# One neighbour product for group 1, chosen by a predicated copy, and a new order of TensorE's turns

## The chip, the cores and the metric

The kernel runs on one core of one Trainium2 chip. The metric is the device time of one execution in microseconds; the figure quoted is the median over the runs. Times inside the kernel are read from one profiled execution and counted in microseconds from the start of its span.

## The reference

The kernel computes one layer of deformable attention over 8 images of 32 channels and 16 x 16 pixels, then a self-attention, then a mixture of 16 small networks. The change touches only the bias of the first attention. Per image and group (G = 2) a convolution predicts an offset for each of 16 sample points; the bias of a query pixel for a point is a bilinear lookup in a table `rpe` at the distance between the two:

```
pos  = offset + ref_points(Hk, Wk)
disp = (qg - pos) * 0.5
bias = grid_sample(rpe_b, disp[..., ::-1])
attn = softmax(einsum('bcm,bcn->bmn', qf, k) * scale + bias)
```

Along x the query grid advances by a little less than one table column per pixel (fifteen sixteenths). So for query column x the lookup is a sum over three neighbouring columns of the shifted table: `here` with weight 1 - |dist|, the next column with weight max(dist, 0), the previous column with weight max(-dist, 0), where dist = frac - x/16. At least one of the last two weights is always zero.

## The kernel before, in words

All 128 partitions hold (image, point) pairs in an order by x position. For each group g, TensorE (the matmuls of L733) writes the table blended along y into PSUM, `row_ps[g]`: 32 rows (16 query rows by 2 heads) at a pitch of 32 columns, 21 columns of which are written. VectorE moves each partition's rows left by a whole number of columns with three predicated copies (`shifted`, L1101), whose mask is one number per partition. GpSimd computes the masks and the weights `tap_next`, `tap_prev`, `tap_both` (their sum) and `tap_here` (L471 to L488).

Then come the products, each of 128 partitions by 512 elements, built by the helper `tap` (its record is L390):

- Group 0: ScalarE copies the shifted rows to SBUF (`win`, L566), and GpSimd forms `left[0]`, `right[0]`, `here[0]` from the copy. Each raises `part_ready[0]`.
- Group 1: VectorE forms `left[1]`, `right[1]`, `here[1]` straight from PSUM, with no wait between them. Each raises `part_ready[1]`.

TensorE turns every product with transposing matmuls (`turn_on`, L761) and accumulates it into `lg_ps`, the logits. `lg_ps` has one bank for each half h of the query pixels. One `turn_on` is two matmuls (one a head) for one product, one group and one half; so the six products make 24 matmuls. Into the same banks go the products of queries and keys (L783), four matmuls of 256 columns a half. Those wait for `k_ready`: the keys are projected by TensorE (`project(0)`, L754), then ScalarE copies them twice, once a head (L571).

The order is the order in which the code is written; each engine takes its instructions strictly in that order, and a wait holds all that stand behind it. On TensorE it is: keys projected; left and right of group 0 for both halves; left of group 1 for both halves; then for each half the four query-key matmuls, right of group 1, here of group 0, here of group 1, and `logits_done`. After that come the projection of the values (`project(1)`, L754) and eight matmuls on x (L797), and then those on the values (L805), which wait for ScalarE's copies of them.

Behind `logits_done` of a half VectorE takes the maximum over a row (L1130) and subtracts it (L1131), ScalarE takes the exponent, VectorE sums and inverts, and the probabilities of half 0 are formed by GpSimd, those of half 1 by VectorE (L398). TensorE's matmuls on `zeros` (L680) fill waits of known length; they keep the engine busy and compute nothing.

Of the kernel before, what the change touches and what calls it, by code (L numbers as in the profile page):

```python
# [9 lines left out]
U32 = mybir.dt.uint32  # L10
ALU = mybir.AluOpType
ACT = mybir.ActivationFunctionType
AX = mybir.AxisListType

P = 128
B, C = 8, 32
IMG = 16
M = IMG * IMG
NHALF = M // P
G = 2  # L20
GC = C // G
HG = 2
# [8 lines left out]
WIN = IMG + 1 + MAXSHIFT  # L31
# [99 lines left out]
def build(nc, x_in, consts_in, weights_in, w1_in, w2_in, out):  # L131
    with ExitStack() as ctx:
# [9 lines left out]
        def bank(n, cols=512):  # L142
            return ps[:, 512 * n:512 * n + cols]
# [67 lines left out]
        tap_next = sb("tap_next", [P, G, IMG])  # L211
        tap_prev = sb("tap_prev", [P, G, IMG])
        tap_both = sb("tap_both", [P, G, IMG])
        tap_here = sb("tap_here", [P, G, IMG])
        win = sb("win", [P, IMG * HG, IMG + 1])

        here = sb("here", [P, G, HG, IMG, IMG])
        left = sb("left", [P, G, HG, IMG, IMG])
        right = sb("right", [P, G, HG, IMG, IMG])
# [56 lines left out]
        row_ps = [ps[:, 1024 * g:1024 * g + 1024].rearrange("p (r c) -> p r c", c=RPAD) for g in range(G)]  # L276
# [8 lines left out]
        sq_ps = [bank(n, M) for n in (4, 2)]  # L285
        y_ps = [bank(n, M) for n in (1, 5)]

        qpad_ps = [bank(2 + g, PADIMG * PADIMG).rearrange("p (y x) -> p y x", y=PADIMG) for g in range(G)]
        q_ps = [qpad_ps[g][:, PAD:PAD + IMG, PAD:PAD + IMG] for g in range(G)]
        att_ps = [bank(2 + h, B * C) for h in range(NHALF)]  # L290
# [51 lines left out]
        k_done, v_done, k_ready, v_ready = sem("k_done"), sem("v_done"), sem("k_ready"), sem("v_ready")  # L342
        vo_done, vo_copied = sem("vo_done"), sem("vo_copied")
        rows_done, win_copied = sem("rows_done"), sem("win_copied")
        shifts_done, left_edge_zeroed = sem("shifts_done"), sem("left_edge_zeroed")
        hat_smp_ready = sem("hat_smp_ready")
        part_ready = [sem(f"part_ready{g}") for g in range(G)]
        logits_done, d_sub_ready = sem("logits_done"), sem("d_sub_ready")
# [39 lines left out]
        def tap(engine, product, g, window, shift, weights, x0=0):  # L388

            return engine.tensor_tensor(  # L390
                product[:, g, :, :, x0:], window[:, :, x0 + shift:IMG + shift].rearrange("p (y h) x -> p h y x", h=HG),
                weights[:, g, x0:].unsqueeze(1).unsqueeze(1).to_broadcast([P, HG, IMG, IMG - x0]), ALU.mult)
# [112 lines left out]
        def _(act):  # L505
# [57 lines left out]
            load_table(LN_EXP_SET)  # L563

            act.wait_ge(shifts_done, 1)
            nc.scalar.activation(win[:, :, :], row_ps[0][:, :, 0:IMG + 1], ACT.Copy).then_inc(win_copied, 1)  # L566

            def copy_heads(w, ready):

# [100 lines left out]
        def _(pe):  # L670
            mm = nc.tensor.matmul

            def nx_rows(nx):

                return slice(nx * P // NK, (nx + 1) * P // NK)
# [11 lines left out]
            for g in range(G):  # L687
                for gi in range(G):
                    pe.wait_ge(xn_ready, gi + 1)
                    last = mm(q_ps[g], wblk[:, 0, gi, g].rearrange("p b o -> p (b o)"),  # L690
                              xn[:, gi].rearrange("p (y x) -> p y x", y=IMG), start=(gi == 0), stop=(gi == G - 1))
# [3 lines left out]
            for h in range(NHALF):  # L695
                for g in range(G):
                    last = nc.tensor.transpose(xnt_ps[:, h, g], xn[:, g, h * P:(h + 1) * P], ident)  # L697
# [22 lines left out]
            for g in range(G):  # L720
                for nx in range(NK):
                    last = mm(tx_ps[nx_rows(nx), g:g + 1], off_blk[:, g].rearrange("p b n -> p (b n)")[:, nx::NK],
                              weight("w_off")[:, 1:2], start=True, stop=True)
# [5 lines left out]
            for g in range(G):  # L729
                for yq in range(4):  # L730
                    pe.wait_ge(hat_rel_ready, yq + 1)
                    for nx, least in enumerate(table_columns()[0]):
                        last = mm(row_ps[g][nx_rows(nx), 8 * yq:8 * yq + 8, 0:WIN],  # L733
                                  minus_hat_rel[:, yq, g * P + nx:(g + 1) * P:NK],
                                  rpe_blk[:, g].rearrange("p k (h c) -> p (k h) c", h=HG)[:, :, least:least + WIN],
                                  start=True, stop=True)
                last.then_inc(rows_done, 1)
# [4 lines left out]
            for g in range(G):  # L742
                for h in range(NHALF):
                    last = mm(xs_ps[:, g], xn_tok[:, h, g], w_smp[:, h, g * P:(g + 1) * P],
                              start=(h == 0), stop=(h == NHALF - 1))
# [12 lines left out]
            def turn_on(part, g, h, start=False):  # L758

                for hh in range(HG):  # L760
                    last = mm(lg_ps[:, h, g, :, hh], part[:, g, hh, 8 * h:8 * h + 8].rearrange("p y x -> p (y x)"),  # L761
                              back_to_n[:, :].rearrange("p (t j) -> p t j", t=NT), start=(start and hh == 0),
                              stop=True, is_transpose=True, skip_group_check=True)
                return last
# [2 lines left out]

            pe.wait_ge(back_to_n_ready, 1)
            pe.wait_ge(txh_ready, 1)
            pe.wait_ge(part_ready[0], 1)  # L770
            for h in range(NHALF):
                turn_on(left, 0, h, start=True)
# [1 line left out]
            for h in range(NHALF):  # L774
                turn_on(right, 0, h)

            pe.wait_ge(part_ready[1], 1)
            for h in range(NHALF):
                turn_on(left, 1, h)
            pe.wait_ge(k_ready, HG)  # L780
            for h in range(NHALF):
                for g in range(G):
                    mm(lg_ps[:, h, g].rearrange("p t k j -> p (t k j)"), q_sb[:, g, h * P:(h + 1) * P],  # L783
                       kv[:, 0, g].rearrange("p t k j -> p (t k j)"), start=False, stop=False, skip_group_check=True)
                pe.wait_ge(part_ready[1], 2)
                turn_on(right, 1, h)
                pe.wait_ge(part_ready[0], 3)
                turn_on(here, 0, h)
                pe.wait_ge(part_ready[1], 3)
                turn_on(here, 1, h).then_inc(logits_done, 1)  # L790

            project(1).then_inc(v_done, 1)
            pe.wait_ge(x_nat_loaded, 16 * B)
# [8 lines left out]
            for outputs, blk in ((voc_ps, woblk_c), (vo_ps, woblk)):  # L802
                for g in range(G):
                    for t in range(NT):
                        last = mm(outputs[:, g, t], kv[:, 1, g, t].rearrange("p k j -> p (k j)"),  # L805
                                  blk[:, g, B4 * t:B4 * t + B4].rearrange("p b o -> p (b o)"),
                                  start=True, stop=True)
# [3 lines left out]
            for h in range(NHALF):  # L811
                pe.wait_ge(d_prob_ready[h], 1)
                for g in range(G):
                    for t in range(NT):
                        first = 2 * B * g + B * t
                        last = nc.tensor.transpose(
                            pt_ps[:, h, g, t], d_prob[:, h, first:first + B].rearrange("p b n -> p (b n)"), ident)
# [4 lines left out]
            for h in range(NHALF):  # L822
                pe.wait_ge(prob_copied, h + 1)
                for t in range(NT):
                    for g in range(G):
                        last = mm(att_ps[h][:, P * t:P * t + P], prob_t[:, h, g, t], vo_c[:, g, t],  # L826
                                  start=False, stop=(g == G - 1), skip_group_check=True)
# [93 lines left out]
            for h in range(NHALF):  # L921
                for b in range(B4, B):
                    last = score(late_ps[:, b - B4, h], b, h, start=(h == 0))
# [3 lines left out]
            for h in range(NHALF):  # L927
                for b in range(B4):
                    last = attend(early_ot_ps, b, h, slice(0, M), start=(h == 0), stop=(h == 1))
            last.then_inc(ot_done, 1)  # L930
            pe.wait_ge(folded_ready, 2)
            for b in range(B4):
                last = add_up(early_sum_ps, b, e_fold[:, b], start=False, stop=True)
# [9 lines left out]
            for q in range(NHALF):  # L943
                queries = slice(P * q, P * q + P)
                pe.wait_ge(exp_ready, NHALF + 2 + q + 1)
                for b in range(B4, B):
                    last = add_up(late_sums_ps[:, q], b, e_tok[:, b, 1, queries], start=False, stop=True)
                last.then_inc(sums_done, 1)
                for b in range(B4, B):
                    last = attend(late_ot_ps[q], b, 1, queries, start=False, stop=True)  # L950
# [47 lines left out]
            for h in range(NHALF):  # L998
                pe.wait_ge(u_copied, 1)
                pe.wait_ge(picked_copied, h + 1)  # L1000
                for b in range(B):
                    last = mm(pool_ps[:, NE * b:NE * b + NE], u[:, h, b, :], picked_t[:, h, b::B],
                              start=(h == 0 and b == 0), stop=(h == NHALF - 1), skip_group_check=True)
# [5 lines left out]
            for q in range(EQ):  # L1009
                last = mm(hid_ps[:, q].rearrange("p e b -> p (e b)"), w1_sb[:, q, :],  # L1010
                          pooled[:, q].rearrange("p e b -> p (e b)"), start=False, stop=True,
                          skip_group_check=True)
# [7 lines left out]
            for e in range(E4):  # L1020
                for q in range(EQ):
                    last = mm(out2_ps[E4 * B * q:E4 * B * q + E4 * B],
                              hidden_blk[:, q, e].rearrange("p f b -> p (f b)"), w2_sb[:, E4 * q + e],
                              start=False, stop=(e == E4 - 1), skip_group_check=True)
# [9 lines left out]
        def _(dve):  # L1034
            steps = [0]

            def link(ins):
                steps[0] += 1
                ins.then_inc(dve_step, 1)
                dve.wait_ge(dve_step, steps[0])  # L1040
# [58 lines left out]
            def shifted(g, width, mask, by):  # L1099

                return nc.vector.copy_predicated(  # L1101
                    row_ps[g][:, :, 0:width], mask.bitcast(U32).unsqueeze(2).to_broadcast([P, IMG * HG, width]),
                    row_ps[g][:, :, by:by + width])

            dve.wait_ge(masks_ready, 1)
            dve.wait_ge(rows_done, 1)
# [12 lines left out]

            dve.wait_ge(shifts_done, 2)  # L1120
            dve.wait_ge(taps_ready, 1)
            dve.wait_ge(left_edge_zeroed, 1)
            tap(nc.vector, left, 1, row_ps[1], -1, tap_prev, 1).then_inc(part_ready[1], 1)
            tap(nc.vector, right, 1, row_ps[1], 1, tap_next).then_inc(part_ready[1], 1)
            tap(nc.vector, here, 1, row_ps[1], 0, tap_here).then_inc(part_ready[1], 1)

            lg_rows = [lg_ps[:, h].rearrange("p g t k (b n) -> p (g t k b) n", n=N) for h in range(NHALF)]
            for h in range(NHALF):
# [162 lines left out]
```

## Time and profile before

| | |
|---|---|
| median of 3 runs | 60.37 us (60.14, 60.37, 61.9) |
| the profiled execution's own time | 59.97 us |
| its span (first to last instruction) | 58.0 us |
| TensorE matmul busy | 50.6 us (87%), 603 matmuls |
| VectorE busy | 36.9 us (64%) |
| ScalarE busy | 29.9 us (52%) |
| GpSimd busy | 18.4 us (32%) |
| transfers | 2.02 MB, 35 GB/s mean |

The profiled execution took 59.97 us, of which 58.0 are the span; 1.97 us lie around it. Busy time counts matmuls as they are modelled: they are pipelined, so the records overlap, and the filling matmuls on `zeros` count too. What a matmul costs in a stream is therefore read from the distance between the starts of two groups, not from its own duration. TensorE's granted clock is at its full level in all 40 slices of the page.

### The profile page before, as it was taken

What the parts mean: (1) busy time and instruction counts of PE and PEld (TensorE: products, weight loads), DVE (VectorE), ACT (ScalarE), POOL (GpSimd) and SP (SyncE); (2) the same over time, 40 slices, a digit from 0 to 9 for tenths busy, and PEclk for the clock granted to TensorE, in tenths of its full rate; (3) what the DMA queues carried; (4) which work ended last, traced back from release to release, by engine and by line L of the source; (5) the groups of instructions that cost most, each with busy time, mean ns of one, the idle gap of its engine ahead of it and who ended that gap; (6) DMA issues with size and microseconds to landing.
All of it is one profiled execution on the core that took longest, in us unless ns stands there. A gap on an engine that the chain in (4) does not pass through costs nothing.

```text
span 58.0 us, 1496 instructions
## 1 busy us (share of the span) xinstructions
PE 50.6 (87%) x603; PEld 41.8 (72%) x603; DVE 36.9 (64%) x95; ACT 29.9 (52%) x66; POOL 18.4 (32%) x41
## 2 busy tenths in 40 slices
PE   3996996999699699999999999979999998979720
PEld 3995894985388579899898986726688675867500
DVE  3478399775659989449994046739267866785320
ACT  0802052787999903104744785197984639801020
POOL 6130089995878899910060000000000000000000
PEclk9999999999999999999999999999999999999999
DMA  0889931110000000000000000000000000000013
GB/s 0 206 183 263 253 105 46 57 41 11 0 0 0 0 11 0 0 0 0 0 0 0 0 0 17 6 0 0 0 0 11 0 0 0 0 0 0 0 44 136
DMA packets 3926, 2.02 MB, mean 35 GB/s; under 512 B 2640, under 2 KB 3792, under 8 KB 3920
## 3 DMA queue, kind: packets, MB, share of 16 engines
q1 hardware_dynamic: 1424, 1.37, 8.1%
q10 hardware_dynamic: 2496, 0.57, 4.7%
q8 instruction: 4, 0.07, 0.5%
q14 instruction: 2, 0.02, 0.1%
HBM read 1.67 MB, written 0.26 MB: 33 GB/s over the span
## 4 chain that ended last, share of the span: by engine, by line
PE 57%; DVE 14%; POOL 8%; ACT 7%; issue 5%; DMA 4%; DVEq 0%; ACTq 0%
PE ps L761 5%; DMA x_sb<-x_rows 4%; PE ps L805 4%; PE ps L754 4%; PE ps L826 4%; PE ps L680 3%; PE ps L884 3%; PE ps L867 3%; PE ps L783 3%; DVE taps L1070 3%; POOL w_smp L486 2%; PE ps L889 2%; ACT e_tok L621 2%; DVE off L1072 2%; PE ps L1030 2%
## 5 line engine op out<-in xcount | busy, mean ns | idle before, releaser
L680 PE MATMUL ps<-zeros 128*128 128x128 bf16 x145 | 11.2, 237 | 1.0 <-DVE zeros L1047 1.0
L680 PEld LDWEIGHTS ps<-zeros 128*128 128x128 bf16 x145 | 10.1, 107 | 1.5 <-DVE zeros L1047 1.0
L511 ACT ACT_TABLE_LOAD x4 | 5.1, 1283 | 1.7 <-PEq L1284 1.6
L621 ACT ACTIVATE e_tok<-ps,cst 128x512 f32<-128x512 f32 (+1 forms) x6 | 4.5, 828 | 1.5 <-PE ps L867 1.5
L1101 DVE COPY_PREDICATED ps<-over,ps 128x608 f32<-128x608 uint32 (+1 forms) x4 | 3.1, 777 | 0.8 <-PE ps L733 0.7
L733 PE MATMUL ps<-rpe_blk,minus_hat_rel 128*32 128x168 f32 x64 | 2.8, 316 | 0.5 <-DVE minus_hat_rel L1097 0.5
L571 ACT ACTIVATE kv<-ps,cst 128x256 f32<-128x256 f32 x4 | 1.7, 472 | 2.8 <-PE ps L754 2.8
L733 PEld LDWEIGHTS ps<-rpe_blk,minus_hat_rel 128*32 128x32 f32 x64 | 2.0, 142 | 1.3 <-issue 0.9
L884 PE MATMUL ps<-e_tok,t 128*32 128x128 f32 (+1 forms) x48 | 2.8, 310 | 0.0
L1148 DVE TENSOR_REDUCE ln_ss<-ln_sq 128x8 f32<-128x264 f32 x2 | 0.9, 428 | 3.0 <-ACT ln_sq L601 3.0
L867 PE MATMUL ps<-t_t 32*128 32x256 f32 x32 | 2.3, 398 | 0.4 <-ACT e_tok L621 0.4
L439 POOL TENSOR_TENSOR wblk<-wts,cst 128x256 f32<-128x256 f32 x3 | 1.9, 628 | 2.2 <-DMA wts<-weights 2.2
L398 POOL TENSOR_TENSOR d_prob<-d_exp,d_rec 128x512 f32<-128x512 f32 x1 | 1.1, 1058 | 4.6 <-DVE d_rec L1137 4.6
L1130 DVE TENSOR_REDUCE d_max<-ps 128x32 f32<-128x512 f32 x2 | 1.4, 692 | 1.7 <-PE ps L761 1.6
L577 ACT ACTIVATE d_exp<-d_sub 128x512 f32<-128x512 f32 x1 | 0.6, 629 | 3.4 <-DVE d_sub L1131 3.4
L690 PE MATMUL ps<-xn,wblk 128*128 128x256 f32 x8 | 2.0, 388 | 0.5 <-DVE xn L1063 0.5
L835 PE MATMUL ps<-prob_t,vo 128*128 128x256 f32 x8 | 2.3, 393 | 0.0
L754 PE MATMUL ps<-xs,wblk 128*128 128x128 f32 x16 | 2.2, 281 | 0.1
L527 ACT ACTIVATE xn_tok<-ps 128x512 f32<-128x512 f32 x1 | 0.6, 598 | 3.2 <-PE ps L697 3.2
L867 PEld LDWEIGHTS ps<-t_t 32*128 32x128 f32 x32 | 1.5, 184 | 0.9 <-issue 0.9
L754 PEld LDWEIGHTS ps<-xs,wblk 128*128 128x128 f32 x16 | 1.9, 191 | 0.3 <-DVE xs L1116 0.3
L1070 DVE TENSOR_TENSOR taps<-ps,wts 128x100 f32<-128x100 f32 x8 | 1.5, 253 | 1.0 <-PE ps L690 1.0
(189 smaller groups left out, 129.9 us busy)
## 6 DMA issues: line engine op xcount, KB each, us to landing
w_sb<-weight ACTq DMA_DIRECT2D x1, 256.0 KB, 6.0
w_sb<-weight SPq DMA_DIRECT2D x1, 256.0 KB, 5.2
x_nat<-x_rows SPq DMA_DIRECT2D x8, 32.0 KB
wts<-weights SPq DMA_DIRECT2D x1, 192.5 KB, 4.5
cst<-shape_consts SPq DMA_DIRECT2D x1, 192.0 KB, 4.1
x_sb<-x_rows SPq DMA_DIRECT2D x1, 128.0 KB, 2.4
x_sb<-x_rows ACTq DMA_DIRECT2D x1, 128.0 KB, 2.6
cst<-shape_consts SPq DMA_DIRECT2D x1, 128.0 KB, 5.0
```

What stands on the lines that cost most here:

```text
L511: nc.scalar.add_instruction(mybir.InstLoadActFuncSet(name=nc.get_next_instruction_name(), act_func_set_id=functions, ins=[], outs=[]))
L621: return nc.scalar.activation(dst, scores, ACT.Exp, bias=const("bound"))
L680: mm(bank(n_bank, P), zeros[:, :], zeros[:, :], start=True, stop=True)
L733: last = mm(row_ps[g][nx_rows(nx), 8 * yq:8 * yq + 8, 0:WIN], minus_hat_rel[:, yq, g * P + nx:(g + 1) * P:NK], rpe_blk[:, g].rearrange("p ...
L754: last = mm(kv_ps[w][:, g], wblk[:, 1 + w, gi, g].rearrange("p b o -> p (b o)"), xs[:, gi], start=(gi == 0), stop=(gi == G - 1))
L761: last = mm(lg_ps[:, h, g, :, hh], part[:, g, hh, 8 * h:8 * h + 8].rearrange("p y x -> p (y x)"), back_to_n[:, :].rearrange("p (t j) -> p ...
L805: last = mm(outputs[:, g, t], kv[:, 1, g, t].rearrange("p k j -> p (k j)"), blk[:, g, B4 * t:B4 * t + B4].rearrange("p b o -> p (b o)"), s ...
L826: last = mm(att_ps[h][:, P * t:P * t + P], prob_t[:, h, g, t], vo_c[:, g, t], start=False, stop=(g == G - 1), skip_group_check=True)
L867: return mm(scores, t1_t[rows, b // B4, h * P:(h + 1) * P], t1_t[rows, b // B4, :], start=start, stop=True, skip_group_check=True)
L884: return mm(out[C * (b % B4):C * (b % B4) + C], t1[:, h, b], e_tok[:, b, h, queries], start=start, stop=stop, skip_group_check=True)
L1070: last = tt(taps[:, g, i].rearrange("p j (a b) -> p j a b", a=KS), conv_view(g, i), dw, ALU.mult)
L1101: return nc.vector.copy_predicated(row_ps[g][:, :, 0:width], mask.bitcast(U32).unsqueeze(2).to_broadcast([P, IMG * HG, width]), row_ps[g][ ...
```

## The change

- `row_ps[g]` keeps its place, but the matmuls of L733 write columns 1 to 21 of a row in place of 0 to 20. A new view `table_ps[g]` starts at column 1, and the shifts, the copy `win` and `here[1]` read through it. Column x of `row_ps[1]` then holds the table's column x - 1, and column x + 2 holds x + 1.
- `left[1]` is dropped. VectorE forms `here[1]` first, waits until it is complete, then copies column x + 2 of `row_ps[1]` over column x wherever `tap_next` is not zero, waits for that copy, and multiplies the result by `tap_both` into `right[1]`. A single product thus carries whichever neighbour has a weight.
- TensorE turns `here[1]` where it turned `left[1]`, now for one half at a time: half 0 runs through to its end (here of group 1, query-key, here of group 0, right of group 1) before anything of half 1 from group 1. The four matmuls that turned `left[1]` are gone. The wait for `left_edge_zeroed` moves from VectorE to TensorE.

```diff
+        table_ps = [row_ps[g][:, :, 1:] for g in range(G)]
...
-            nc.scalar.activation(win[:, :, :], row_ps[0][:, :, 0:IMG + 1], ACT.Copy).then_inc(win_copied, 1)
+            nc.scalar.activation(win[:, :, :], table_ps[0][:, :, 0:IMG + 1], ACT.Copy).then_inc(win_copied, 1)
...
-                        last = mm(row_ps[g][nx_rows(nx), 8 * yq:8 * yq + 8, 0:WIN],
+                        last = mm(row_ps[g][nx_rows(nx), 8 * yq:8 * yq + 8, 1:1 + WIN],
...
+            pe.wait_ge(left_edge_zeroed, 1)
...
-            pe.wait_ge(part_ready[1], 1)
-            for h in range(NHALF):
-                turn_on(left, 1, h)
-            pe.wait_ge(k_ready, HG)
-            for h in range(NHALF):
+            def by_keys(h):
+
                 for g in range(G):
                     mm(lg_ps[:, h, g].rearrange("p t k j -> p (t k j)"), q_sb[:, g, h * P:(h + 1) * P],
                        kv[:, 0, g].rearrange("p t k j -> p (t k j)"), start=False, stop=False, skip_group_check=True)
-                pe.wait_ge(part_ready[1], 2)
-                turn_on(right, 1, h)
-                pe.wait_ge(part_ready[0], 3)
-                turn_on(here, 0, h)
-                pe.wait_ge(part_ready[1], 3)
-                turn_on(here, 1, h).then_inc(logits_done, 1)
+
+            pe.wait_ge(part_ready[1], 1)
+            turn_on(here, 1, 0)
+            pe.wait_ge(k_ready, HG)
+            by_keys(0)
+            pe.wait_ge(part_ready[0], 3)
+            turn_on(here, 0, 0)
+            pe.wait_ge(part_ready[1], 2)
+            turn_on(right, 1, 0).then_inc(logits_done, 1)
+            turn_on(here, 1, 1)
+            by_keys(1)
+            turn_on(here, 0, 1)
+            turn_on(right, 1, 1).then_inc(logits_done, 1)
...
-                    row_ps[g][:, :, 0:width], mask.bitcast(U32).unsqueeze(2).to_broadcast([P, IMG * HG, width]),
-                    row_ps[g][:, :, by:by + width])
+                    table_ps[g][:, :, 0:width], mask.bitcast(U32).unsqueeze(2).to_broadcast([P, IMG * HG, width]),
+                    table_ps[g][:, :, by:by + width])
...
-            dve.wait_ge(left_edge_zeroed, 1)
-            tap(nc.vector, left, 1, row_ps[1], -1, tap_prev, 1).then_inc(part_ready[1], 1)
-            tap(nc.vector, right, 1, row_ps[1], 1, tap_next).then_inc(part_ready[1], 1)
-            tap(nc.vector, here, 1, row_ps[1], 0, tap_here).then_inc(part_ready[1], 1)
+            tap(nc.vector, here, 1, table_ps[1], 0, tap_here).then_inc(part_ready[1], 1)
+            dve.wait_ge(part_ready[1], 1)
+            link(nc.vector.copy_predicated(
+                row_ps[1][:, :, 0:IMG], tap_next[:, 1].bitcast(U32).unsqueeze(1).to_broadcast([P, IMG * HG, IMG]),
+                row_ps[1][:, :, 2:IMG + 2]))
+            tap(nc.vector, right, 1, row_ps[1], 0, tap_both).then_inc(part_ready[1], 1)
```

## Rows read from the trace of the kernel before

**Rows 1.** The page: shares of the chain that ended last; instruction transfers.
```profile
PE 57%; DVE 14%; POOL 8%; ACT 7%; issue 5%; DMA 4%; DVEq 0%; ACTq 0%
...
q8 instruction: 4, 0.07, 0.5%
```

**Rows 2.** Chain in order of time: start us, us, what.
```profile
22.61 1.31 PE ps L761 x12
...
26.97 0.89 PE ps L754 x8
27.86 0.89 PE ps L797 x8
28.75 0.04 issue
```

**Rows 3.** Timeline of TensorE's matmuls: start us, us from first to last, instruction [idle before].
```profile
21.46 1.16 PE L754 MATMUL ps<-xs,wblk 128*128 128x128 f32 x8
22.45 0.60 PE L761 MATMUL ps<-back_to_n,left 128*128 128x128 f32 x4
22.89 0.60 PE L761 MATMUL ps<-back_to_n,right 128*128 128x128 f32 x4
23.32 0.60 PE L761 MATMUL ps<-back_to_n,left 128*128 128x128 f32 x4
23.76 1.03 PE L783 MATMUL ps<-kv,q_sb 128*128 128x256 f32 x4
24.63 0.38 PE L761 MATMUL ps<-back_to_n,right 128*128 128x128 f32 x2
24.84 0.60 PE L761 MATMUL ps<-back_to_n,here 128*128 128x128 f32 x4
25.28 1.03 PE L783 MATMUL ps<-kv,q_sb 128*128 128x256 f32 x4
...
26.80 1.06 PE L754 MATMUL ps<-xs,wblk 128*128 128x128 f32 x8
```

**Rows 4.** Timeline of VectorE, the copies, the products of group 1 and the maxima.
```profile
21.32 0.72 DVE L1101 COPY_PREDICATED ps<-odd,ps 128x544 f32<-128x544 uint32 x1
22.07 0.66 DVE L390 TENSOR_TENSOR left<-ps,tap_prev 128x480 f32<-128x480 f32 x1
22.65 0.68 DVE L390 TENSOR_TENSOR right<-ps,tap_next 128x512 f32<-128x512 f32 x1
23.25 0.68 DVE L390 TENSOR_TENSOR here<-ps,tap_here 128x512 f32<-128x512 f32 x1
25.48 0.69 DVE L1130 TENSOR_REDUCE d_max<-ps 128x32 f32<-128x512 f32 x1 [1.56 <-PE ps L761]
...
26.21 0.69 DVE L1131 TENSOR_TENSOR d_sub<-ps,d_max 128x512 f32<-128x512 f32 x1
...
27.00 0.69 DVE L1130 TENSOR_REDUCE d_max<-ps 128x32 f32<-128x512 f32 x1
```

**Rows 5.** Timeline of ScalarE: the copies of keys and values.
```profile
22.65 0.84 ACT L571 ACTIVATE kv<-ps,cst 128x256 f32<-128x256 f32 x2 [2.45 <-PE ps L754]
...
27.90 0.84 ACT L571 ACTIVATE kv<-ps,cst 128x256 f32<-128x256 f32 x2 [0.33 <-PE ps L754]
```

**Rows 6.** Timeline of GpSimd: weights, products of group 0, later work.
```profile
19.91 0.22 POOL L488 TENSOR_SCALAR tap_here<-tap_both 128x32 f32<-128x32 f32 x1
...
21.39 1.20 POOL L390 TENSOR_TENSOR right<-win,tap_next 128x512 f32<-128x512 f32 x1
22.54 1.22 POOL L390 TENSOR_TENSOR here<-win,tap_here 128x512 f32<-128x512 f32 x1
23.72 1.19 POOL L439 TENSOR_TENSOR woblk_c<-wo_c,cst 128x256 f32<-128x256 f32 x2
```

**Rows 7.** Groups by shape, 15 to 31 us: count | busy us, mean ns | idle before.
```profile
L1101 DVE COPY_PREDICATED ps<-over,ps 128x608 f32<-128x608 uint32 x2 | 1.6, 793 | 0.7 <-PE ps L733 0.7
L1101 DVE COPY_PREDICATED ps<-odd,ps 128x544 f32<-128x544 uint32 x2 | 1.4, 725 | 0.0
```

## The prediction

> **What bounds the kernel now.** I read the page first: TensorE holds 57% of the chain of work that ended last and VectorE 14% [rows 1]. Then the chain in order of time around the edit: it enters TensorE before 22.45 us and stays there, without a gap, through the 24 turning matmuls, the eight query-key matmuls, the projection of the values and the matmuls on x, until 28.75 [rows 2]. Then the timelines, engine by engine. On TensorE each group begins where the one before it has issued [rows 3]: the turns of 128 columns go at four in 0.44 us (22.45 to 22.89), 0.109 each; the query-key matmuls of 256 columns at four in 0.87 (23.76 to 24.63), 0.218 each. Check: 24 x 0.109 + 8 x 0.218 = 4.36 us, and the stretch from 22.45 to 26.80 is 4.35. So no product is late for its turn today: VectorE ends its last product at 23.93 [rows 4] and GpSimd at 23.76 [rows 6], while the first turn of a `here` starts at 24.84 [rows 3]. VectorE then sits idle 1.56 us until the logits of half 0 are done [rows 4]. In this stretch the number of matmuls sets the time, not VectorE.
>
> **Turns removed.** Four turns of `left[1]` go: 4 x 0.109 = 0.44 us off a stream without gaps. Nothing is added to TensorE but one more wait, `left_edge_zeroed`, for a memset issued at the start: nothing.
>
> **The new order, first the keys.** `left[1]` stood ahead of the query-key matmuls with four turns, and now two turns of `here[1]` stand there. So the first query-key matmul is due at 22.45 + 0.44 + 0.43 + 0.22 = 23.54 in place of 23.76. It needs both ScalarE copies of the keys, which end at 22.65 + 0.84 = 23.49 [rows 5]. That is the one place where the cover is used up. TensorE resumed 0.04 to 0.05 after ScalarE's end at the same kind of wait (copies of the values end at 27.90 + 0.84 = 28.74 [rows 5], the chain has 0.04 of issue before the next matmul [rows 2]); and a group that starts behind a wait pays for its first weight load in the open: the projection is eight matmuls in 1.16 us behind a wait and the same eight in 1.06 in a stream [rows 3]. So the matmul comes at 23.54 plus 0.10. Bounds: 0, if load and wait just fit, to 0.2, if both the restart and a little lateness of ScalarE count. I take 0.10, since the load must be issued ahead of the matmul and so before 23.49. Moving a wait past anything else: behind it stand only TensorE's own turns.
>
> **VectorE.** Before: three products, starts 0.58 and 0.60 apart, end at 23.93. After: `here[1]` from 22.07 to 22.75 (its weights are there since 20.13 [rows 6]). The added waits make each next step begin after the end of the last; with such a wait the maximum and the subtraction stand 0.73 apart at 0.69 each [rows 4], so 0.04 a wait. The copy: 608 elements take 793 ns and 544 take 725 [rows 7], 1.06 ns an element, so 512 take 0.69 us. It would run 22.79 to 23.48, and the last product 23.52 to 24.20; the turn can see it at 24.24. That is 0.27 later than VectorE ends today. The reads at other column offsets cost nothing: `right` at +1 and `here` at 0 both take 0.68 [rows 4]. The mask is new in kind, one word for each element and no longer one a partition; no row shows that. Lower bound 0.64 (a little under a product's 0.68), upper bound GpSimd's product of the same size, 1.22 us [rows 6]; I take 0.69, because all else about the copy is as in [rows 7].
>
> First the rows: products without a wait between them start closer together than they last (0.60 against 0.68), steps with one start 0.73 apart [rows 4]. The Trainium skill (VectorE: DVE Perf Modes, The DRAIN you can't avoid) says that the next operation cannot issue before the pipeline is empty and that a semaphore in between costs nothing extra. By that the two new waits would be free and the last product would be ready at 23.95, 0.25 us sooner than I have it; by the rows each costs 0.13 against an unlinked start. I follow the rows; the sum stays the same by either, the cover of the last product (below) would be 0.74 by the one and is 0.49 by the other.
>
> **TensorE's timetable after.** Left and right of group 0 to 23.32; `here[1]` half 0 to 23.54 (ready at 22.75); restart to 23.64; query-key to 24.51; `here[0]` to 24.73 (GpSimd done 23.76, cover 0.75); `right[1]` to 24.95 (needed at 24.73, ready at 24.24, cover 0.49). Half 1: 0.22 + 0.87 + 0.22 + 0.22 = 1.53, to 26.47. The projection of the values starts at 26.47 in place of 26.80: 0.33 sooner (0.44 of turns, less 0.10 of restart, rounded). Half 0 is issued to its end at 24.95 in place of 24.84 + 0.44 = 25.28, also 0.33 sooner.
>
> If `right[1]` were late, all of half 1 and the projection of the values would queue behind it, and VectorE and ScalarE with them. The cover of 0.49 is what the copy may grow by at no cost: up to 0.69 + 0.49 = 1.18 us. At the upper bound of 1.22 it would be 0.04 late, and with the restart behind the wait (0.10) the loss is 0.14.
>
> **After that.** The softmax starts with the maximum, which waited for TensorE; the second maximum starts at 27.00, as TensorE's last turn is done. ScalarE's copies of the values waited 0.33 for TensorE [rows 5]. Other inputs have long been there: GpSimd's `woblk_c` ends at 24.91 [rows 6], needed at 28.4 after the change. So the whole tail shifts by 0.33; nothing in it has a time of its own. The shift is carried in full.
>
> **Sum.** -0.44 (turns) + 0.10 (restart) + 0 (VectorE, covered) = -0.33 us on the profiled execution: span 58.0 to 57.7, own time 59.97 to 59.64. The median stands 0.40 above that execution, so I carry the difference over: 60.37 - 0.33 = 60.04, say 60.0.
>
> **Rivals.**
> 1. *The copy is held up while GpSimd works.* GpSimd's `here[0]` runs from 22.54 to 23.76 [rows 6], right across the place of the copy. Were the copy to wait for its end, it would run 23.78 to 24.47, the product to 25.19, and TensorE would resume at 25.24 plus the restart of 0.10: 0.61 late, a net loss of 0.28, 60.65 us: slower than before. It decides from a copy that ends over 0.49 after its plan, and turns the sign from about 0.7 (0.49 of cover and 0.33 of gain, less the restart). Against it: `left[1]` and `right[1]` ran at 0.66 and 0.68 beside GpSimd's products, from PSUM and one SBUF operand [rows 4], as the copy does. Beside that, the Trainium skill (SBUF — State Buffer) has VectorE and GpSimd take an exclusive lock on a shared port pair only where VectorE runs a two-port mode or has two SBUF inputs; by its word this rival falls away, and the trace agrees for the products. Chance 0.08. A mask read so slowly that the copy doubles to 1.38 belongs here too: 0.20 late and a restart, near 60.3.
> 2. *The gain is given back.* Transfers of instructions run through the kernel (four in one queue [rows 1]); if the tail depended on one of them, or a wait of the tail had a fixed end, the result would be 60.37. The chain shows no such step in the tail from 22.61 to 28.75. Chance 0.08.
> 3. *The keys are not in the way.* No restart: the full 0.44, 59.93 us. Chance 0.2; it lies in the forecast's own range.
> 4. *Something much larger.* Four turns are all that goes, and VectorE's shorter program is not shorter in time. For 1.2 us to be gained, twelve turns would have to vanish: 0.02. For 1.2 us to be lost the copy would have to take about 2.7 us or a chain of surprises come together: 0.04.
> The forecast has the rest, 0.58; with rival 3, 0.78.
>
> **How the numbers follow.** Two per cent of 60.37 is 1.21 us, about what a measurement of this kernel can tell from no change. My forecast, rivals 1, 2 and 3 all lie within it: 0.08 + 0.08 + 0.2 + 0.58 = 0.94, of which I move a little to each side since the three runs themselves spread from 60.14 to 61.9: same 0.92, faster 0.03, slower 0.05. The range: from the full gain of 0.44 below the lowest execution shown (59.97 - 0.44 = 59.5) to rival 1 (60.65), 59.5 to 60.7.
>
> **What the changed profile would show.** 20 turning matmuls in place of 24 before the values' projection, which starts near 26.45. A small idle ahead of the first query-key matmul, released by ScalarE's key copies. A predicated copy of 512 elements near 0.69 us at 22.8. The last product of group 1 ending near 24.2, and no wait of TensorE for it. `d_max` of half 0 starting near 25.15, half 1 near 26.67. I would be wrong if the copy takes over 1.2 us, if TensorE idles before `right[1]`, or if the tail from the values' projection to the end is not as long as before.

## The result and the profile after

The changed kernel takes 59.86 us in the median of 15 runs, the one before 60.67 in the median of 15 beside it. The ratio, changed over before, is 0.9909, 95% interval [0.9882, 0.9935]: a gain of 0.9%, 0.55 us, within two per cent but clear of noise. (Some executions of most kernels here take about one or two us longer, most of them with a longer span at a lower granted clock and some, of kernels with 24 turns only, with more time around the span; the ratios leave them out, the medians do not.)

The changed stretch on TensorE is as the timetable had it. Timeline of the changed kernel's matmuls, as [rows 3]:

```profile
21.71 1.16 PE L755 MATMUL ps<-xs,wblk 128*128 128x128 f32 x8
22.70 0.60 PE L762 MATMUL ps<-back_to_n,left 128*128 128x128 f32 x4
23.14 0.60 PE L762 MATMUL ps<-back_to_n,right 128*128 128x128 f32 x4
23.57 0.38 PE L762 MATMUL ps<-back_to_n,here 128*128 128x128 f32 x2
23.80 1.13 PE L782 MATMUL ps<-kv,q_sb 128*128 128x256 f32 x4
24.77 0.38 PE L762 MATMUL ps<-back_to_n,here 128*128 128x128 f32 x2
24.98 0.38 PE L762 MATMUL ps<-back_to_n,right 128*128 128x128 f32 x2
25.20 0.38 PE L762 MATMUL ps<-back_to_n,here 128*128 128x128 f32 x2
25.42 1.03 PE L782 MATMUL ps<-kv,q_sb 128*128 128x256 f32 x4
26.29 0.38 PE L762 MATMUL ps<-back_to_n,here 128*128 128x128 f32 x2
26.50 0.38 PE L762 MATMUL ps<-back_to_n,right 128*128 128x128 f32 x2
26.72 1.06 PE L755 MATMUL ps<-xs,wblk 128*128 128x128 f32 x8
```

The keys' projection (the first row) starts 0.25 us later in this execution than in that of before. That is no effect of the edit: the input tile `x_sb` landed later, so that VectorE's first work on it starts at 3.46 in place of 3.18, and the kernel before, run once more below, starts its keys' projection later still. So all comparisons below use distances from that row. **From the keys' projection to the values' projection it is 26.72 - 21.71 = 5.01 us, against 26.80 - 21.46 = 5.34 in [rows 3]: 0.33 less.** The first four query-key matmuls take 0.97 from start to next start where the second four take 0.87. The rows of the weight loads (PEld) show why. Before, the first load stood 0.11 ahead of its matmul at 23.76; in the changed kernel load and matmul start together at 23.80, so this load is in the open. First row the kernel before, second the changed one:

```profile
23.65 0.73 PEld L783 LDWEIGHTS ps<-kv,q_sb 128*128 128x128 f32 x4
```

```profile
23.80 0.73 PEld L782 LDWEIGHTS ps<-kv,q_sb 128*128 128x128 f32 x4
```

VectorE and ScalarE of the changed kernel in the same stretch, as [rows 4] and [rows 5]:

```profile
22.33 0.69 DVE L391 TENSOR_TENSOR here<-ps,tap_here 128x512 f32<-128x512 f32 x1
22.90 0.84 ACT L572 ACTIVATE kv<-ps,cst 128x256 f32<-128x256 f32 x2 [2.42 <-PE ps L755]
23.05 0.70 DVE L1130 COPY_PREDICATED ps<-tap_next,ps 128x512 f32<-128x512 uint32 x1
23.79 0.69 DVE L391 TENSOR_TENSOR right<-ps,tap_both 128x512 f32<-128x512 f32 x1
25.40 0.69 DVE L1138 TENSOR_REDUCE d_max<-ps 128x32 f32<-128x512 f32 x1 [0.93 <-PE ps L762]
26.92 0.69 DVE L1138 TENSOR_REDUCE d_max<-ps 128x32 f32<-128x512 f32 x1
```

The copy with a mask for each element takes 0.70 us. The keys are copied at 22.90 + 0.84 = 23.74, and TensorE's first query-key matmul starts at 23.80. VectorE ends its last product at 24.48, 0.50 ahead of its turn at 24.98, and still waits 0.93 for TensorE before the first maximum. The two maxima start 3.69 and 5.21 after the keys' projection, against 4.02 and 5.54 before: both 0.33 sooner.

The tail is as long as before. ScalarE's last copy starts 55.42 - 26.72 = 28.70 after the values' projection, before 55.50 - 26.80 = 28.70. First row the kernel before, second the changed one:

```profile
55.50 0.38 ACT L665 ACTIVATE y_sb<-ps 128x256 f32<-128x256 f32 x1 [2.34 <-PE ps L1030]
```

```profile
55.42 0.38 ACT L666 ACTIVATE y_sb<-ps 128x256 f32<-128x256 f32 x1 [2.34 <-PE ps L1036]
```

### The profile page after: what moved, and what is told of

Read it like the earlier page. It is cut to its first block, busy times and chain, and to the rows that moved or that the text cites. A ratio compares the mean times of both kernels' runs of the same rounds, so it can differ in the third digit from the quotient of the medians.

```text
span 58.0 us, 1489 instructions
## 1 busy us (share of the span) xinstructions
PE 50.5 (87%) x599; PEld 41.6 (72%) x599; DVE 37.0 (64%) x95; ACT 29.9 (52%) x66; POOL 18.3 (32%) x41
## 4 chain that ended last, share of the span: by engine, by line
PE 56%; DVE 14%; POOL 8%; ACT 7%; issue 5%; DMA 5%; DVEq 0%; ACTq 0%
DMA x_sb<-x_rows 5%; PE ps L762 4%; PE ps L811 4%; PE ps L755 4%; PE ps L832 4%; PE ps L681 3%; PE ps L890 3%; PE ps L782 3%; PE ps L873 3%; DVE taps L1076 3%; POOL w_smp L487 2%; PE ps L895 2%; ACT e_tok L622 2%; DVE off L1078 2%; PE ps L1036 2%
## 5 line engine op out<-in xcount | busy, mean ns | idle before, releaser
L782 PE MATMUL ps<-kv,q_sb 128*128 128x256 f32 x8 | 2.2, 392 | 0.0
```

## The experiments

"Turns" counts the turning matmuls. "Distance" is always from the start of the keys' projection to the start of the values' projection on TensorE; "first maximum" is the start of `d_max` of half 0, from the same origin. "Outside" is the median of an execution's time less its span, over the executions that the ratios count (their number in brackets); spans are on record to 0.1 us.

| kernel | turns | ratio to before | distance | first maximum | outside |
|---|---|---|---|---|---|
| before | 24 | 1 | 5.34 | 4.02 | 1.98 (63 executions) |
| before once more | 24 | 1.0014 [0.9976, 1.0052] | 5.35 | 4.03 | in the row above |
| offset only | 24 | 0.9996 [0.9956, 1.0036] | 5.35 | 4.03 | 1.93 (10) |
| order only | 24 | 1.0041 [0.998, 1.0102] | 5.45 | 3.91 | 2.43 (6) |
| left turns dropped | 20 | 0.9984 [0.9887, 1.0082] | 5.29 | 3.97 | 1.79 (4) |
| changed | 20 | 0.9909 [0.9882, 0.9935] | 5.01 | 3.69 | 1.79 (21) |
| last product 0.31 late | 20 | 0.9894 [0.9823, 0.9965] | 5.02 | 3.70 | 1.80 (4) |
| last product 0.73 late | 20 | 0.9952 [0.9909, 0.9995] | 5.34 | 4.02 | 1.82 (9) |
| both halves first | 20 | 0.9848 [0.9798, 0.9898] | 4.91 | 3.81 | 1.82 (11) |
| one turn ahead | 20 | 0.9868 [0.9819, 0.9918] | 4.91 | 3.70 | 1.81 (12) |

The tail, from the values' projection to ScalarE's last copy, is 28.69 to 28.71 in every trace in which the granted clock stays full up to that copy, whatever the kernel. So what the distance gains is carried to the end.

What the runs had to decide. *Theory:* TensorE's stream is the path, ScalarE's key copies are a floor under the first query-key matmul (it cannot start sooner), and VectorE's last product has a cover near half a microsecond (it may end that much later at no cost). *Rivals:* the number of turns alone counts; the earlier softmax of half 0 is what counts; VectorE's end counts.

### Left turns dropped

```diff
             pe.wait_ge(part_ready[1], 1)
-            for h in range(NHALF):
-                turn_on(left, 1, h)
             pe.wait_ge(k_ready, HG)
```

> The kernel before without the four turns of left[1]; the product is still formed but never reaches the logits. Theory (the keys are the floor): the query-key matmuls are then due 0.44 us sooner, but ScalarE's key copies end only 0.27 before their old place, so with 0.04 to 0.05 of signalling and 0.10 of an open weight load they start just 0.12 sooner; the distance from the keys' projection to the values' projection on TensorE falls from 5.34 to 5.22 us, and the time by 0.1. Rival (the number of turns alone sets the time): the distance falls by the whole 0.44 to 4.90.

The chain of waits of this kernel in order of time, and TensorE's rows:

```profile
22.69 0.85 ACT kv L571 x2
23.54 0.14 issue
```

```profile
21.50 1.16 PE L754 MATMUL ps<-xs,wblk 128*128 128x128 f32 x8
23.68 1.10 PE L781 MATMUL ps<-kv,q_sb 128*128 128x256 f32 x4
24.61 0.38 PE L761 MATMUL ps<-back_to_n,right 128*128 128x128 f32 x2
26.79 1.06 PE L754 MATMUL ps<-xs,wblk 128*128 128x128 f32 x8
```

The distance is 5.29. The chain now leaves TensorE and runs through ScalarE's key copies. Of 0.44 us of work taken away only 0.05 arrives. The rival is out: it needed 4.90. I had expected a gain of 0.12. The first query-key matmul does start 0.12 sooner (23.68 - 21.50 = 2.18 after the keys' projection, before 2.30), 0.14 behind ScalarE's end; but its group then takes 0.93 to the next start where 0.87 is the rule, and these 0.06 I had not counted. From the whole time nothing can be told: its interval reaches over no change.

### Order only

```diff
+            turn_on(left, 1, 0)
+            pe.wait_ge(k_ready, HG)
+            by_keys(0)
...
+            turn_on(here, 1, 0).then_inc(logits_done, 1)
+            turn_on(left, 1, 1)
+            by_keys(1)
```

> The kernel before with its three products and 24 turns, but half 0 run through to its end before half 1, as in the change. Theory: two turns fewer stand before the keys, so the restart of 0.10 us is paid and nothing saved: distance from the keys' to the values' projection 5.44 against 5.34; the maximum of half 0 starts some 0.11 sooner. Time the same within 0.1. Rival (the order alone brings the gain, since half 0's softmax starts sooner): time 0.3 to 0.5 lower.

Distance 5.45, first maximum 0.11 sooner, ratio 1.0041. TensorE's rows:

```profile
22.27 1.16 PE L754 MATMUL ps<-xs,wblk 128*128 128x128 f32 x8
24.36 1.13 PE L780 MATMUL ps<-kv,q_sb 128*128 128x256 f32 x4
25.33 0.38 PE L761 MATMUL ps<-back_to_n,right 128*128 128x128 f32 x2
27.72 1.06 PE L754 MATMUL ps<-xs,wblk 128*128 128x128 f32 x8
```

The four query-key matmuls reach 0.97 to the next start, as in the changed kernel: the restart of 0.10 is paid and there is no turn less to set against it. An earlier half 0 buys nothing: the tail from the values' projection is 28.70, as before. So neither half of the change gives its gain alone: fewer turns in the old order run into the keys, the new order without fewer turns costs 0.10, and together they give 0.33.

### Both halves of `here[1]` first, and one turn ahead

```diff
             turn_on(here, 1, 0)
+            turn_on(here, 1, 1)
             pe.wait_ge(k_ready, HG)
```

```diff
             turn_on(here, 1, 0)
+            turn_on(here, 1, 1, heads=[0])
             pe.wait_ge(k_ready, HG)
```

Each leaves out, behind the first query-key matmuls, what it has put in front. Both were run twice, the second time with the changed kernel on the same chip:

> The changed kernel, but both halves of here[1] are turned before the wait for the keys, as left[1] was before. Theory: the four turns cover the wait, no restart, distance 4.91 us (5.34 less 0.44) against 5.01 in the changed kernel; the maximum of half 0 starts 0.11 later than in the changed kernel. Time 0 to 0.1 below the changed kernel, 0.4 below before. Rival (half 0's softmax is what counts): 0.1 above the changed kernel.

> The changed kernel with a single turn of half 1 (here[1], first head) moved ahead of the wait for the keys. Theory: that turn fills the 0.10 us in which TensorE would wait and load weights in the open; distance 4.91 to 4.95 us against 5.01, half 0's maximum no more than 0.02 later; time up to 0.1 below the changed kernel. Rival (the restart is no cost of the wait but of the keys' own lateness): distance stays 5.01.

> Both halves of here[1] turned ahead of the wait for the keys, again. Theory: distance 4.91 us as with one turn ahead, but the maximum of half 0 starts 0.11 later; the start of the probabilities' turns shows whether that is lost: if half 0's softmax is the later of the two paths there, they start 4.0 us and not 3.88 after the values' projection. Time between the changed kernel and the one with one turn ahead.

> The changed kernel with one turn of here[1] of half 1 ahead of the wait for the keys, again, now on the same chip as the changed kernel. Theory: distance 4.91 us, 0.1 below the changed kernel in the median time, so 0.983 to 0.990 of before. Rival (the 0.1 is lost in the tail): same time as the changed kernel.

> The changed kernel on the same chip as the two before, for comparison. Theory: distance 5.01 us; the span 0.3 below before's in the median of the undisturbed runs, and about 0.1 above the kernel with one turn ahead.

The first runs gave 0.9846 [0.9782, 0.991] (both halves first) and 0.9843 [0.9787, 0.9899] (one turn ahead). Side by side the medians are 59.71 and 59.70 us, and 59.80 for the changed kernel (its ratio 0.9888 [0.9834, 0.9943]). The distance is 4.91 in both, 0.10 less than in the changed kernel. TensorE and VectorE with both halves first:

```profile
21.38 1.16 PE L755 MATMUL ps<-xs,wblk 128*128 128x128 f32 x8
23.69 1.03 PE L782 MATMUL ps<-kv,q_sb 128*128 128x256 f32 x4
25.19 0.69 DVE L1138 TENSOR_REDUCE d_max<-ps 128x32 f32<-128x512 f32 x1 [1.04 <-PE ps L762]
26.29 1.06 PE L755 MATMUL ps<-xs,wblk 128*128 128x128 f32 x8
30.17 1.14 PE L822 MATMUL ps<-cst,d_prob 128*128 128x128 f32 x8
```

And with one turn ahead:

```profile
21.78 1.16 PE L755 MATMUL ps<-xs,wblk 128*128 128x128 f32 x8
23.98 1.03 PE L782 MATMUL ps<-kv,q_sb 128*128 128x256 f32 x4
25.48 0.69 DVE L1139 TENSOR_REDUCE d_max<-ps 128x32 f32<-128x512 f32 x1 [0.93 <-PE ps L762]
26.69 1.06 PE L755 MATMUL ps<-xs,wblk 128*128 128x128 f32 x8
30.57 1.12 PE L823 MATMUL ps<-cst,d_prob 128*128 128x128 f32 x8
```

The query-key group is back at 1.03 for four: one turn of 0.109 is enough to cover wait and load. It is only just enough: in this trace the key copies end at 23.82, the weight load starts at 23.87, and the matmul at 23.98, right behind the turns. With both halves first the maximum starts at 3.81, 0.11 later than with one turn ahead, and yet the probabilities' turns start 30.17 - 26.29 = 3.88 after the values' projection in both. So the softmax of half 0 still has at least 0.11 to spare; the rival that it decides is out. The 0.10 stands in the rows, and the tails behind it are 28.70 (both halves first) and 28.71; the medians agree with it (59.70, 59.71, 59.80), though the intervals of the ratios overlap. Both are the best versions of this study, and I cannot tell the two apart.

### The last product made late

```diff
+            link(tt(d_sub[:, 1, 0:8], row_ps[1][:, 0:8, 0:IMG],
+                    tap_both[:, 1].unsqueeze(1).to_broadcast([P, 8, IMG]), ALU.mult))
             tap(nc.vector, right, 1, row_ps[1], 0, tap_both).then_inc(part_ready[1], 1)
```

The second kernel has 32 in place of 8.

> The changed kernel with one more small product (128 elements a partition, into a buffer that is written anew later) on VectorE between the predicated copy and the last product, waited for. It costs VectorE about 0.3 us. Theory (cover of 0.46 to 0.49): the last product is ready near 24.8 on the clock of the changed trace, its turn starts at 24.98, nothing moves: distance 5.01 us, time as the changed kernel. Rival (VectorE's end already decides): 0.3 us longer.

> The same with a product of full size, 0.73 us more on VectorE. Theory: 0.73 less the cover of 0.46, that is 0.27 late, and 0.10 for a restart behind the wait: distance 5.38 us against 5.01, time about 0.37 above the changed kernel, so the change's whole gain is gone. Rival (a cover larger than I read): distance under 5.2.

The small product: 0.29 us in VectorE's timeline, the last product ends at 24.15 + 0.69 = 24.84, its turn starts at 25.03, nothing moves, distance 5.02. The full one (the granted clock of this execution falls only past 53 us):

```profile
21.80 1.16 PE L755 MATMUL ps<-xs,wblk 128*128 128x128 f32 x8
23.88 0.69 DVE L1133 TENSOR_TENSOR d_sub<-ps,tap_both 128x512 f32<-128x512 f32 x1
24.60 0.69 DVE L391 TENSOR_TENSOR right<-ps,tap_both 128x512 f32<-128x512 f32 x1
24.86 0.38 PE L762 MATMUL ps<-back_to_n,here 128*128 128x128 f32 x2
25.35 0.44 PE L762 MATMUL ps<-back_to_n,right 128*128 128x128 f32 x2
25.62 0.38 PE L762 MATMUL ps<-back_to_n,here 128*128 128x128 f32 x2
27.14 1.06 PE L755 MATMUL ps<-xs,wblk 128*128 128x128 f32 x8
```

The turns of `right` were due at 24.86 + 0.22 = 25.08, start at 25.35, and the next pair follows 0.27 later where 0.22 is the rule: 0.27 late and 0.05 to 0.06 of restart. Distance 5.34, the gain in this stretch is gone. The cover is between 0.3 and 0.73, and by these rows 0.73 - 0.27 = 0.46. I had expected 5.38: the restart ahead of turns of 128 columns costs about half of what it costs ahead of the query-key matmuls.

### Offset only

Only the new column of the table's rows and the readers' views, with the three products and the order of before:

```diff
-                        last = mm(row_ps[g][nx_rows(nx), 8 * yq:8 * yq + 8, 0:WIN],
+                        last = mm(row_ps[g][nx_rows(nx), 8 * yq:8 * yq + 8, 1:1 + WIN],
```

> The kernel before with the table's rows one column further right in PSUM and every reader moved with them, nothing else. Theory: no cost and no gain, the predicated copies keep 793, 762 and 725 ns, the matmuls of the table 316 ns in the mean, distance 5.34 us, time the same within 0.1. Rival (part of the measured 0.55 comes from the new alignment): time 0.2 lower.

Ratio 0.9996, distance 26.91 - 21.56 = 5.35, and VectorE's shifts take 0.72 to 0.80 us each, as before. The offset is free.

### The changed kernel and the one before, once more

> The changed kernel once more, beside the others on the same chip. Theory: distance 5.01 us, time 0.33 below before in the stretch; the 0.55 measured first holds about 0.2 that lies outside this stretch or is spread of the runs. Rival: the difference is 0.5 to 0.6 again, and the missing 0.2 has a cause that the trace of one execution did not show.

The changed kernel again: 0.9899 [0.9847, 0.9952], distance 26.69 - 21.68 = 5.01. In the trace beside the two kernels above it is 26.64 - 21.63 = 5.01 too. So the distance repeats to the hundredth. The difference in whole time is again about 0.6, though by itself this interval reaches down to 0.29 and does not exclude 0.33.

> The kernel before, unchanged, once more. It asks where the rest of the measured gain (0.55 to 0.65 us, against 0.33 in the distance) comes from. If the one trace of before is a quick execution of it, this one starts its keys' projection or ends its tail later than that trace: a span of 58.2 to 58.6 in place of 58.0, with the distance still 5.34. If the distance itself varies (above 5.34), the stretch of the change holds more than I read from one execution. Against itself the ratio should lie within 0.5% of 1.

The kernel before, once more: distance 27.28 - 21.93 = 5.35, span 58.5 in place of 58.0. Its matmul and ScalarE rows:

```profile
0.97 4.98 PE L680 MATMUL ps<-zeros 128*128 128x128 bf16 x45 [0.97 <-DVE zeros L1047]
21.93 1.16 PE L754 MATMUL ps<-xs,wblk 128*128 128x128 f32 x8
27.28 1.06 PE L754 MATMUL ps<-xs,wblk 128*128 128x128 f32 x8
55.99 0.38 ACT L665 ACTIVATE y_sb<-ps 128x256 f32<-128x256 f32 x1 [2.34 <-PE ps L1030]
```

The first execution shown had:

```profile
0.97 4.10 PE L680 MATMUL ps<-zeros 128*128 128x128 bf16 x45 [0.97 <-DVE zeros L1047]
```

The tail is 55.99 - 27.28 = 28.71, the same. Of the 0.49 by which ScalarE's last copy is later, 0.47 lie ahead of the keys' projection. The same 45 filling matmuls took 4.98 us and not 4.10, and the chain of this execution runs through them into the first real matmuls. But most of the delay is there without them. The input tile landed 0.34 later, as VectorE's first row on it shows, here in the first execution and in this one:

```profile
3.18 0.43 DVE L1052 BATCH_NORM_STATS2 stats<-x_sb 128x6 f32<-128x256 f32 x1 [1.14 <-DMA x_sb<-x_rows]
```

```profile
3.52 0.43 DVE L1052 BATCH_NORM_STATS2 stats<-x_sb 128x6 f32<-128x256 f32 x1 [1.49 <-DMA x_sb<-x_rows]
```

The first real matmul starts the same 0.34 later (5.88 against 5.54), and the first four of them, up to VectorE's next step, take 0.17 longer (1.31 against 1.14). The trace of before on which the prediction rests had a quick start.

## Why the prediction was right

- **Turns removed, -0.44.** Right: the 24 turns became 20 at the same 0.109. With the restart covered the distance falls by 0.43 (5.34 to 4.91).
- **The restart at the keys, +0.10.** Right in place and size: 0.97 against 0.87 for four query-key matmuls, and one turn moved ahead takes it away. It has another form than the sign that I gave. There is no idle ahead of the first query-key matmul and the chain does not pass through ScalarE there: the matmul starts at 23.80, where 23.79 was due, and the 0.10 lies inside its group. The bound of 0.2 was not needed here, but the kernel with the turns dropped reached it: 0.14 from ScalarE's end to the matmul and 0.06 inside the group.
- **VectorE, covered.** Right. The copy took 0.70 (forecast 0.69), the last product ended 0.30 later than the old last one (forecast 0.27), cover 0.46 by experiment and 0.50 by the row (forecast 0.49). The waits between VectorE's steps cost what [rows 4] said: starts 0.72 and 0.74 apart, where the unlinked products stood 0.58 and 0.60. The sentence of the Trainium skill that I set against it (VectorE: DVE Perf Modes, The DRAIN you can't avoid), that a semaphore costs nothing extra, is not borne out here: it would have made the cover 0.74. I had left out that the same section lets a next operation start earlier when it is not held, which is what the unlinked products do.
- **The copy held up beside GpSimd (rival 1).** Did not happen: it ran 23.05 to 23.75 while GpSimd's last product was running:

```profile
22.84 1.21 POOL L391 TENSOR_TENSOR here<-win,tap_here 128x512 f32<-128x512 f32 x1
```

  What the Trainium skill states (SBUF — State Buffer, Who interferes with whom), that a VectorE instruction with at most one SBUF input and outside the two-port modes does not contend with GpSimd, agrees with the 0.70.
- **The gain given back (rival 2).** Did not happen: the tail is 28.70 before and after.
- **No restart (rival 3).** Did not happen in the changed kernel, and is what moving one turn ahead brings.
- **The sum.** The stretch gave -0.33, as forecast, in three traces of the changed kernel. The measured ratio, 0.0065 to 0.0118 below 1, is 0.39 to 0.71 us of 60.4, so 0.33 is just outside. The term that was mis-sized is the last: "I carry the difference over", that is, nothing but this stretch would change. Over the executions of this study that the ratios count, the median span went from 58.4 (63 executions of before) to 58.0 (21 of the changed kernel), in line with 0.33; the time outside the span went from 1.98 to 1.79 as well. 0.33 + 0.19 = 0.52 lies within what was measured.
- **Luck.** The forecast of 60.0 started from a median of only three executions, one of them at 61.9. That it was a sound base (60.43 is the median over the 63) was luck, and it does not make up for the 0.19 that the sum lacks.

What stays open is why the time outside the span fell by 0.19. The table has a pattern: all six kernels with 20 turns stand at 1.79 to 1.82, also the one that only drops turns from the old kernel and the one whose distance is back at 5.34; those with 24 turns stand at 1.93 or more. Single executions show what is behind the medians. Every kernel has some at 1.75 to 1.80. What differs is how many stand above 1.86: 80 of all 110 executions with 24 turns, up to 2.96, and 6 of all 78 with 20 turns, up to 2.16. But three of these 6 belong to the 10 of the kernel with the last product 0.73 late, so the number of turns may not be all. That kernel keeps a ratio of 0.9952 with no gain left in the stretch; its shorter time outside, 0.16 in the medians, covers about half of these 0.29 us, and the rest is within the interval. So the time outside goes for the most part with the program and not with the distance. Why is not known: a smaller program, or its place in memory, would be a guess, and no run tested it.

## What to carry to other kernels

On an engine without gaps, count the instructions that go, then look for the first wait that they had been hiding: here four turns were worth 0.05 us in the old order and 0.33 in the new one. A single instruction whose input is already there, put in front of such a wait, gives back the restart, here 0.10 us. Compare distances between two instructions inside the trace before comparing whole times: the distance repeated within 0.01 us in every trace of the same kernel, while the start of the keys' projection differed by up to 0.89 (22.27 and 21.38 in the two traces with both halves first).

## What the runs showed that I had not expected

- The restart of TensorE behind a wait is not one number: 0.10 ahead of 256-column matmuls that start at their due time, 0.05 to 0.06 ahead of turns, and in the kernel with the turns dropped, where TensorE's last turn had been through for 0.31, 0.14 from ScalarE's end to the matmul and 0.06 more in its group.
- The 45 filling matmuls at the start took 4.10 us in one execution and 4.98 in another of the same kernel, with the granted clock at 1.00 in all slices of that part in both. Up to 4 us both executions run alike, with 10, 13 and 12 matmuls in the three stretches of one us from 1 to 4; from 4 to 5 us it is 19 in the first and 13 in the other. So the rate changes at a moment that differs from one execution to the next, and the clock row does not show it. What sets it is open.
- In some executions the granted clock falls near the very end. In that of the kernel with the offset alone the last four matmuls took 1.65 us, in before 1.13:

```profile
54.43 1.65 PE L1031 MATMUL ps<-chosen,out_blk 128*128 128x256 f32 x4 [0.42 <-DVE out_blk L1241]
```

The page's clock row of that execution has the last slices at 7, 5 and 5 tenths (half speed is the level of 1.2 GHz):

```profile
PEclk9999999999999999999999999999999999999755
```

It adds spread to whole times that no edit in the middle of the kernel explains.
